# Attention outputs by query: the exps as TensorE's weights, v with a column of ones streamed, in a four-layer transformer kernel

## The reference, cut to what matters

```python
scores = jnp.einsum('bqhd,bkhd->bhqk', Q, K) / np.sqrt(HEAD_DIM).astype(np.float32)
attn = jax.nn.softmax(scores, axis=-1)
attn_out = jnp.einsum('bhqk,bkhd->bqhd', attn, V).reshape(B, N, D_MODEL)
attn_out = attn_out @ Wo + bo
x = x + gate1 * attn_out
h = _layernorm(x) * (1.0 + scale2) + shift2
ff = jax.nn.gelu(h @ W1 + b1, approximate=False) @ W2 + b2
return x + gate2 * ff
```

## Time and profile before

| | |
|---|---|
| Median of 2 runs | 1180.39 us (1178.21 to 1182.58) |
| The profiled execution | 1179.05 us |
| Its span, first to last instruction | 1177.3 us |
| Mean granted TensorE clock | 0.981 |
| Busy: TensorE matmul / weight load | 91% / 72% |
| Busy: VectorE / ScalarE / GpSimd | 66% / 49% / 15% |

### The profile page before, as it was taken

The page is one execution under the profiler, slowest core; times in us unless marked ns, Lnnn a source line. Parts: engine busy times, 40 slices in busy tenths (PEclk is TensorE's granted clock), DMA queues, the critical chain, the costliest instruction groups (busy, mean ns, idle before and its releaser), DMA issues.

```text
span 1177.3 us, 21434 instructions
## 1 busy us (share of the span) xinstructions
PE 1073.8 (91%) x7540; PEld 852.4 (72%) x7540; DVE 779.3 (66%) x2091; ACT 574.3 (49%) x1140; POOL 174.9 (15%) x288
## 2 busy tenths in 40 slices
PE   5799999999999999999999978888888999999895
PEld 4667777788787787877888755555556787877664
DVE  4476667776677666777666677766768766667622
ACT  4245565554553445544456444444445545655441
POOL 3011011110113101101101101111114110101100
PEclk9799999999999999999999999999999999999988
DMA  7732333222345223331233433333434123332200
GB/s 235 252 113 65 92 109 109 81 63 72 109 154 188 67 83 109 109 103 56 70 106 112 136 110 109 109 109 109 132 130 145 56 75 108 117 117 67 78 2 17
DMA packets 102714, 123.20 MB, mean 105 GB/s; under 512 B 8992, under 2 KB 96032, under 8 KB 101600
## 3 DMA queue, kind: packets, MB, share of 16 engines
q1 hardware_dynamic: 102048, 121.73, 33.1%
q10 hardware_dynamic: 576, 0.30, 0.1%
HBM read 85.16 MB, written 35.78 MB: 103 GB/s over the span
## 4 chain that ended last, share of the span: by engine, by line
PE 64%; DVE 13%; DMA 9%; ACT 4%; issue 3%; SPq 3%; POOL 1%; ACTq 1%; DVEq 0%; POOLq 0%
PE dense L1175 13%; PE o_banks L1252 8%; PE s_bank L1199 8%; PE dense L1161 8%; DMA q_stack<-max_t 6%; PE st_bank L1236 5%; PE o_banks L1135 4%; PE dense L1106 4%; DVE xn L773 3%; PE o_banks L1121 3%; DVE neg_max L801 3%; PE o_banks L1085 2%; PE o_banks L1260 2%; DMA k_stack<-qk_dram 2%; ACT probs L609 2%
## 5 line engine op out<-in xcount | busy, mean ns | idle before, releaser
L609 ACT ACTIVATE probs<-st_bank 128x512 f32<-128x512 f32 (+1 forms) x512 | 264.1, 568 | 173.2 <-PE st_bank L1236 121.4
L801 DVE TENSOR_REDUCE neg_max<-s_bank 128x2 f32<-128x512 f32 x384 | 255.6, 684 | 103.1 <-PE s_bank L1199 100.7
L1199 PE MATMUL s_bank<-k_stack,q_stack 96*128 96x256 f32 (+1 forms) x1024 | 234.3, 320 | 19.1 <-DMA k_stack<-qk_dram 10.7
L1199 PEld LDWEIGHTS s_bank<-k_stack,q_stack 96*128 96x128 f32 x1024 | 170.9, 194 | 60.3 <-DVE neg_max L801 16.7
L1175 PE MATMUL dense<-w_sb,hid 128*128 128x256 f32 x768 | 204.9, 381 | 0.0
L1236 PE MATMUL st_bank<-q_stack,k_stack 98*128 98x512 f32 x384 | 153.9, 474 | 13.3 <-DMA q_stack<-max_t 10.6
L444 POOL TENSOR_TENSOR veps<-mv,eps_c 128x2 f32<-128x2 f32 x65 | 14.3, 220 | 958.2 <-DVE mv L767 891.5
L1175 PEld LDWEIGHTS dense<-w_sb,hid 128*128 128x128 f32 x768 | 128.9, 189 | 9.6 <-issue 0.4
L597 ACT ACTIVATE hid<-dense,vec 128x256 f32<-128x256 f32 x192 | 80.6, 471 | 107.9 <-PE dense L1161 107.9
L1252 PE MATMUL o_banks<-probs,v_aug 128*32 128x256 f32 (+1 forms) x2048 | 123.0, 382 | 10.1 <-DVE xg L840 5.8
L1106 PE MATMUL dense<-ht,w_sb 128*128 128x256 f32 x512 | 127.3, 388 | 3.9 <-ACT ht L551 1.3
(11 more groups left out here) (124 smaller groups left out, 1467.9 us busy)
## 6 DMA issues: line engine op xcount, KB each, us to landing
q_stack<-qk_dram SPq DMA_DIRECT2D x192, 128.0 KB, 2.9
k_stack<-qk_dram SPq DMA_DIRECT2D x96, 256.0 KB, 4.1
par_sb<-par_dram SPq DMA_DIRECT2D x32, 512.0 KB, 5.3
qk_dram<-q_hi SPq DMA_DIRECT2D x32, 256.0 KB, 2.1
qk_dram<-q_lo SPq DMA_DIRECT2D x32, 256.0 KB, 2.1
qk_dram<-k_hi SPq DMA_DIRECT2D x32, 256.0 KB, 2.1
qk_dram<-k_lo SPq DMA_DIRECT2D x32, 256.0 KB, 2.1
w_sb<-w SPq DMA_DIRECT2D x3, 1280.0 KB, 7.6
```

What stands on the lines that cost most here:

```text
L609: nc.scalar.activation(probs[p % 4][:, kt, :, q0:N], src, ACT.Exp, scale=SCORE_SCALE[l]).then_inc(p_sb, 1)
L801: nc.vector.tensor_reduce(neg_max[:, qt, 2 * p:2 * p + 2], split3(bank[:]), AX.X, ALU.max, negate=True).then_inc(s_max, 1)
L1199: ins = mm(bank[:, e * N:e * N + k1], q_stack[g.par][0:KB, 2 * p + e, qt * P:(qt + 1) * P].bitcast(F32R), k_stack[g.par][0:KB, p, 0:k1].bi ...
```

## The change

Now the exps are the weights and v is streamed. `v_aug` holds 17 columns for each head: v and one column of ones. `values(g, *pairs)` runs for one pair at a time: for each of 2 heads and 2 query tiles it accumulates over the key tiles (only those up to the query tile in the causal layer) a matmul with 128x128 weights `probs[p % 4][:, kt, e, qt tile]` and 17 streamed columns. The result has the queries on the partitions, so `out_copy`, `out_turn` and `o_sb` are gone, and `out_norm` reads the output bank itself, one reciprocal and one multiply for each half. `exps` of pair p wait for the outputs of pair p - 4 alone. On GpSimd both `addend`s stand behind `power(n, 0)` and a wait for VectorE's norm `xn1`. On TensorE the value blocks, and in the short branch also the projection and the first scores of `a`, stand in other places, and VectorE's order follows them.

```diff
-        v_aug = [sb(f"v_aug{i}", [P, T, H, 2 * HD]) for i in range(2)]
+        v_aug = [sb(f"v_aug{i}", [P, T, H, HD + 1]) for i in range(2)]
...
-                    addend(c, 1, xg2)
                     if g.reg is None and g.off % B == 1 and g.layer > 0 and HAS_MLP[g.layer]:
                         split_w1(g.layer)
-                wait(pool, par_ld, g.count(16, 16))
                 if n.exists:
+
                     power(n, 0, ln1_mv, ln1_veps, ln1_rstd)
+                    wait(pool, xn1_done, n.count(1, 1))
+                if c.exists:
+                    wait(pool, xn2_done, c.count(1, 1))
+                    wait(pool, par_ld, g.count(16, 16))
+                    addend(c, 1, xg2)
+                    wait(pool, xg2, c.count(1, 1))
                 else:
-                    wait(pool, xg2, c.count(1, 1))
-                    wait(pool, xn2_done, c.count(1, 1))
+                    wait(pool, par_ld, g.count(16, 16))
                 addend(g, 0, xg1)
...
-            def out_copy(g, h):
-
-                wait(act, o_ps, g.count(2, h + 1))
-                wait(act, ot_ps, g.count(2, h))
-                nc.scalar.activation(o_sb[:], o_banks[:, :, 0:N], ACT.Copy).then_inc(o_copy, 1)
...
-                    if p % 4 == 0:
-                        wait(act, o_ps, g.count(2, p // 4))
+                    wait(act, o_ps, g.count(PAIRS, p - 3))
...
             def out_norm(g, h):
 
-                wait(dve, ot_ps, g.count(2, h + 1))
-                o5 = o_banks[:, :, N:2 * N].rearrange("p i (t h d) -> p i t h d", t=T, h=4)
-                wait(dve, ao_sb, g.count(4, 2 * h))
-                nc.vector.reciprocal(rec[:], o5[:, :, :, :, HD]).then_inc(rec_sb, 1)
+                wait(dve, o_ps, g.count(PAIRS, (h + 1) * PAIRS // 2))
+                o = half_of_outputs(h)
+                wait(dve, ao_sb, g.count(2, h))
+                nc.vector.reciprocal(rec[:], o[:, :, :, HD]).then_inc(rec_sb, 1)
                 wait(dve, rec_sb, g.count(2, h + 1))
                 if h == 0:
                     wait(dve, aot_ps, g.count(1, 0))
-                for i in range(2):
-                    c0 = 4 * HD * (2 * h + i)
-                    dst = ao[:, :, c0:c0 + 4 * HD].rearrange("p t (h d) -> p t h d", h=4)
-                    nc.vector.tensor_tensor(dst, o5[:, i, :, :, 0:HD],
-                                            rec[:, i].unsqueeze(3).to_broadcast([P, T, 4, HD]), ALU.mult).then_inc(ao_sb, 1)
+                c0 = h * D // 2
+                dst = ao[:, :, c0:c0 + D // 2].rearrange("p t (h d) -> p t h d", h=H // 2)
+                nc.vector.tensor_tensor(dst, o[:, :, :, 0:HD], rec[:].unsqueeze(3).to_broadcast([P, T, H // 2, HD]),
+                                        ALU.mult).then_inc(ao_sb, 1)
...
-            def values(g, h):
-
-                if h == 0:
-                    wait(pe, v_sb, g.count(1, 2) if g.ahead(1).exists else g.count(1, 1))
-                    if g.off > 0:
-                        wait(pe, x1_done, g.count(1, 0))
-                else:
-                    wait(pe, ao_sb, g.count(4, 2))
-                wait(pe, p_sb, g.count(16, 8 * h + 8))
-                for i in range(2):
-                    for kt in range(T):
-                        q0 = P if CAUSAL[g.layer] and kt else 0
-                        for j in range(4):
-                            pr = probs[2 * i + j // 2]
-                            ins = mm(o_bank[i][32 * j:32 * j + 32, q0:N], v_aug[g.par][:, kt, 8 * h + 4 * i + j, :],
-                                     pr[:, kt, j % 2, q0:N], start=kt == 0, stop=kt == T - 1)
-                ins.then_inc(o_ps, 1)
-
-            def out_turn(g, h):
-                wait(pe, o_copy, g.count(2, h + 1))
-                for i in range(2):
-                    for t in range(T):
-                        ins = tr(o_bank[i][:, N + t * P:N + (t + 1) * P], o_sb[:, i, t * P:(t + 1) * P], ident[:])
-                ins.then_inc(ot_ps, 1)
+            def values(g, *pairs):
+
+                for p in pairs:
+                    if p == 0:
+                        wait(pe, v_sb, g.count(1, 1))
+                        if g.off > 0:
+                            wait(pe, x1_done, g.count(1, 0))
+                    if p == PAIRS // 2 and g.ahead(1).exists:
+                        wait(pe, v_sb, g.count(1, 2))
+                    wait(pe, p_sb, g.count(16, 2 * p + 2))
+                    o = o_bank[p // 4][:, 0:T * (H // 2) * (HD + 1)].rearrange("p (t h d) -> p t h d", t=T, h=H // 2)
+                    for e in range(2):
+                        for qt in range(T):
+                            keys = qt + 1 if CAUSAL[g.layer] else T
+                            for kt in range(keys):
+                                ins = mm(o[:, qt, 2 * (p % 4) + e], probs[p % 4][:, kt, e, qt * P:(qt + 1) * P],
+                                         v_aug[g.par][:, kt, 2 * p + e], start=kt == 0, stop=kt == keys - 1)
+                    ins.then_inc(o_ps, 1)
```

More of the change, by code:

```diff
@@ L538, in value_copy @@
                 wait(act, v_ps, a.count(1, 1))
-                wait(act, o_ps, a.count(2, 2 - 2 * 2))
+                wait(act, o_ps, a.count(PAIRS, PAIRS - 2 * PAIRS))
                 if a.reg is None and a.off < 2:
@@ L1006, in step @@
                     max_split(a, 0)
+                    out_norm(g, 1)
                     max_copy(a, 0)
@@ L1090, in ht1_t @@
                 wait(pe, v_sb, a.count(1, 0))
-                wait(pe, ao_sb, a.count(4, 4 - 2 * 4))
+                wait(pe, ao_sb, a.count(2, 2 - 2 * 2))
                 transposed(o_bank[1], xn1, ht1_ps)
@@ L1126, in ao_turn @@
             def ao_turn(g):
-                wait(pe, ao_sb, g.count(4, 4))
+                wait(pe, ao_sb, g.count(2, 2))
                 transposed(o_bank[0], ao, aot_ps)
@@ L1281, in step @@
                     score_t(g, 2)
+                    values(g, 0)
+                    score(g, 12)
                     ht2_t(c, a)
-                    score(g, 12)
                     if inputs:
@@ L1286, in step @@
                     score_t(g, 3)
+                    values(g, 1)
                     if inputs:
@@ L1368, in step @@
                     values(g, 0)
+                    score(a, 0)
+                    values(g, 1)
+                    score(a, 1)
+                    values(g, 2)
+                    score(a, 2)
+                    values(g, 3)
                     if modulated:
```

141 lines of the change are left out of this document (65 added, 76 removed).

## The result

The kernel after takes 1599.53 us (median of 2 runs, 1587.78 to 1611.27) against 1180.39 us: 1.352 times the time before, 95% interval 1.344 to 1.360. The forecast was 1520 us with a range of 1365 to 1640. So the direction and the range held, and the forecast was 80 us too low. The other run took 1587.78 us at 0.859. Each ratio compares fast runs: a run over 1.5% above the fastest of its kernel, at a lower granted clock, is left out of it.

What follows compares the result with a forecast made beforehand. TensorE, busy 1073.8 of 1177.3 us, was taken as the bound. 1179.05 + 267.5 - 23 - 36 = 1387.5 us at full clock, plus 131 for the clock, gave 1519, rounded to 1520 us; range 1365 to 1640.

Steps and rivals of the forecast that it cites:

- 267.5 - 23 - 36: Whole kernel at full clock: 267.5 us net TensorE work added, less 23 idle in MLP steps and 36 in steps without.
- The price of a record: New output matmuls on TensorE: 0.106 us per record, 128 records per non-causal step and 96 per causal one.
- what goes (4.60 us): TensorE's old output blocks and turns, two of each per non-causal step: 2 x (1.86 + 0.44) = 4.60 us removed.
- The idle time of MLP steps: 23 steps with an MLP: 1.0 us idle TensorE each, nearly the 22.7 us norm wait; 23 us given back once.
- Of 5 us I take 4: 9 steps without an MLP: TensorE's added work fills 4 of 5 us idle time each, 36 us given back.
- The clock: Value stretches at lower granted clock: 11 us in each of 9 layer 2-type steps, 1.4 in 23 MLP steps; 131 us.
- the row at 58 us: Kernel before, 58 to 62 us: TensorE busy with weight loads and little streaming, yet granted clock 0.57 on average.
- The choice of 11: Steps without an MLP: 11 of a possible 18 us lost to half clock, since the fall comes some us in.
- B: Rival: the clock holds because value blocks are spread between products and scores; 1390 us, chance 0.29.
- C: Rival: loads of short matmuls overlap, each record costs its stream alone, 0.015 us; 1096 us, chance 0.04.
- D: Rival: GpSimd's two sums become late and come onto the path, adding 82 us; about 1600 us, chance 0.07.
- What it would show: Signs: records every 0.106 us, weight path fullest, PEclk falling in layer 2, longer waits, MLP steps 44 to 46 us.

Runs made afterwards that it cites:

- stream112: The changed kernel with 112 instead of 17 columns streamed past each weight load, same loads and order: 1420.4 us, ratio 1.202.
- pool_alone: The kernel before with only GpSimd's two sums moved as in the change: 1180.05 us, ratio 0.997.
- pool_undone: The changed kernel with GpSimd's two sums back in their old places: 1585.53 and 1587.02 us, ratio 1.340; also 1609.76 and 1614.52 us.
- order112: The changed kernel with 112 columns streamed and, in steps without an MLP, maxima turns, first scores and VectorE's last norm reordered: 1387.76 us, ratio 1.173.
- stream64: The changed kernel with 64 instead of 17 columns streamed past each weight load: 1543.25 and 1576.45 us.
- stream32: The changed kernel with 32 instead of 17 columns streamed past each weight load: 1573.88 us, ratio 1.333.
- grouped: The changed kernel with its eight value blocks per step gathered into two of four pairs each: 1766.95 us, ratio 1.493.
- before_bf16: The kernel before with exps and v stored as bf16, in the old layout: 1171.23 us, ratio 0.990.

## Why the prediction was right in its direction and 92 us short

The span grew by 432 us. `stream112` has the change's loads and order and a clock of 0.986, so it splits the sum: 1417.8 - 1177.3 = 240.5 us nearly at full clock, and 1609.5 - 1417.8 = 191.7 us of clock (some 168 in the change's other run). The prediction had 208.5 (267.5 - 23 - 36) and 131: 32 and 61 us too little.

- **The price of a record** (0.106 us, taken from L1064) was right: 0.105 and 0.106. The number of them was right too, and with what goes (4.60 us) the sum fits: MLP steps take 44.03 us at full clock, where 36 + 9 - 1 = 44 was worked out, and causal ones 40.9 to 41.1. The Trainium skill, page "TensorE: Matmul & The Clock Gate", section "LDWEIGHTS (loading the stationary operand)", puts a load's nanoseconds at its columns divided by 1.2; 128 columns are an estimated 107 ns by it, and these rows agree. The gap for 1 to 64 columns, weighed in the prediction from the section "Back-to-back issue gap" of the same Trainium skill page, is given there for a matmul without its load; the section says that in a stream of loads and matmuls both set the spacing, and these rows agree: with a new fp32 load for each record 0.106 us stand in place of 25 ns.
- **The idle time of MLP steps** (23 us, given back once) was right in kind and a little small: TensorE idled 32.5 us in the 23 MLP steps before, 1.4 us each and not 1.0, and 3.9 in those of `stream112`; in most it idles 0.02 us or so. That GpSimd's sums would stop delaying the norm was right in the norm's own length (`pool_alone`). As a cause of the gain it was not needed: `pool_undone` has it too.
- **"Of 5 us I take 4": failed.** The steps without an MLP gave nothing back. In the eight steps of layer 2 TensorE idled 37.4 us before, 38.8 in the change and 42.9 in `stream112`. In `stream112` they took 314.9 us against 239.3, which is 9.5 us each more, for 9.0 us of added work. The prediction filled idle time by amount, as if added work slid into any gap. But the code order put score(a, 0) behind one value block, where k_stack had not landed, and left both turns of the maxima in front of VectorE's results. `order112` changed that and got 32 us: 1386.0, beside the 1385.8 that the terms give on the span (1177.3 + 267.5 - 23 - 36). That these agree to 0.2 us is luck: layer 2's steps grew by 5.8 us each where 5.0 was worked out, the part up to the turn of step 0 by 8.9 for 5, and the last seven MLP steps by 47 us for 56, partly because the kernel before had a clock of 0.980 there and `order112` 1.00.
- **The clock: right in mechanism, too small in size.** The falls come in the value stretches of layer 2, as the row at 58 us had led to expect. Step by step, the change against `stream112`: layer 2 lost 126.7 us in 8 steps, 15.8 each, where 11 was taken and 18 was the bound; from the start to the turn of step 0's outputs it lost 15.9 where 11 was taken; the steps with an MLP lost 49.1, 2.1 each, where 1.4 was taken. The choice of 11 let the fall come some us into the stretch and end with the step. The second half was wrong: the clock stays low over the next step's scores and first products, L1091 x16 with 6.26 us instead of 3.69 (read from start to end in the change and in a step of `stream64` at full clock). The stretch itself was a little short as well: 18 us were worked out, and in `stream112` TensorE is busy for 19.83 us of it.
- **Rivals.** B (the clock holds, 1390 us) describes `order112`, not the change. (For it stood "no fall in MLP steps before"; the last of them had 0.86.) C (loads overlap, 0.015 us per record) is false in fp32. Its turning point of 0.036 us is passed in bf16 with 0.027 and half as many records, where the change costs 1% instead of 35%. It does not gain there: layer 2's eight steps take 275.3 us against 239.3, by the clock (0.70 to 0.77) and by 13 us more idle time, with TensorE waiting 62.8 us for k_stack in the whole kernel (10.7 before). D (GpSimd's sums late) is false: undoing that part changed nothing that could be measured.
- **What it would show.** Record distances, the PEclk slices and the longer waits of VectorE and ScalarE came as named. The weight path did not become the fullest row, with 86% beside 95% for the matmuls, though it is busy for 7.78 of the 8 us from 1058 us on. MLP steps came at 43.9 to 48.6 us (one at 56.0, causal ones mostly 41.0). The 45 us for steps of layer 2 was wrong, with 52.6 to 58.9.

What stays open: why one MLP step fell to 0.77 while its neighbours had 0.93 and 0.90, why with 64 columns two steps of layer 2 held and six did not, and what the order of `order112` would do with 17 columns. With the same 3840 loads the span times the mean clock is nearly one number (1358 for the change, 1362 for `stream32`, 1370 for `stream64`, 1361 for `grouped`, 1372 for `order112`; 1398 for `stream112` with its waits). So a run's time follows from how long the clock was low, but these rows don't give when it falls.

## What to carry to other kernels

Before exps or other large operands become the weights, price the loads: here, with 17 to 112 columns per load, an fp32 matmul cost its two loads and the stream was free, so the layout that streams many columns past weights loaded once won, though it needs a copy and a turn. Count TensorE's clock as a second price of the same edit: here a busy engine that loaded weights and streamed 17 columns past each load lost half its speed, and it stayed slow into the work behind; a stretch of before where loads stand alone shows it. Added work fills idle time only if it stands in front of the wait: read each wait's place in the new order, not its sum.

## What the runs showed of the hardware that was not expected

- Useless streaming can pay: 112 columns instead of 17 past each weight load took 179 us off (1599.53 to 1420.4), with each load at 0.106 us either way.
- The clock can fall where work is taken away. `before_bf16` does 2.6 us less per step and has 0.925 instead of 0.981.
- A bf16 record with a 128x128 load and 17 columns takes 0.027 us (the median over blocks of 8 at full clock; 0.025 in the fastest), an fp32 record 0.106, though both load 128x128. The Trainium skill, page "TensorE: Matmul & The Clock Gate", section "Weight-path perf modes — Fast Weight Load (FWL) and DoubleRow", says that the fast load gives nothing for fp32 and that it reads two bf16 weights at a time; it puts the gain at four times in theory for fp8 and at about two as measured. These rows agree on fp32 and show 0.106 / 0.027 = 3.9 from fp32 to bf16; the measurement decides.
- Half clock doubles the time of a weight load too: 0.105 to 0.204 us.
- The order alone, with the same instructions, moved the mean clock from 0.844 to 0.769 (`grouped`).
- A GpSimd sum beside VectorE's norm makes the norm's median 972 ns instead of 410, and taking it away gained nothing that could be measured.
